# Inverse roots of a three-round attention by Newton steps on VectorE, with TensorE's fillers and the keys' statistics placed elsewhere

## What is computed

```python
def _ln(x, w, eps=1e-05):
    m = jnp.mean(x, axis=-1, keepdims=True)
    v = jnp.var(x, axis=-1, keepdims=True)
    return (x - m) * jax.lax.rsqrt(v + eps) * w

for it in range(3):
    ql = qcur[:, :, :E] @ Wlq.T + blq
    kl = kcur[:, :, :E] @ Wlk.T + blk
    vl = vcur[:, :, :E] @ Wlv.T + blv
    qs = _ln(ql, lnc_w) * tscale
    ks_ = _ln(kl, lnd_w)
    logits = jnp.einsum('bhqd,bhkd->bhqk', qs, ks_) * sm_scale
    ai = jnp.einsum('bhqk,bhkd->bhqd', jax.nn.softmax(logits, axis=-1), vl)
    iter_out = jnp.zeros_like(qcur).at[:, :, :E].set(ai)     # only the first E = 16 positions
    diff = jnp.mean(jnp.abs(iter_out - prev))
    attn_out = jnp.where(done, attn_out, iter_out)
    done = done | (diff < thr + fac * diff) & (it > 0)
    prev, qcur, kcur, vcur = iter_out, qcur + iter_out, kl, vl
```

## Time and profile before

| | us |
|---|---|
| median of 3 runs (2586.53 to 2589.68) | 2589.26 |
| profiled execution, its own time | 2587.26 |
| its span, first to last instruction | 2585.5 |
| TensorE busy (share of the span) | 2471.9 (96%) |
| VectorE | 2179.0 (84%) |
| ScalarE | 1852.1 (72%) |
| GpSimd | 1123.0 (43%) |
| opening stage, its last VectorE instruction to end | 151.4 |
| the next stage's first instructions | 151.65 |

### The profile page before, as it was taken

One profiled execution on the slowest core, in us unless ns is written; L12 is line 12 of the kernel. 1 busy time (PEld: TensorE's weight loads), 2 busy tenths in 40 slices (PEclk: granted clock), 3 DMA queues, 4 the chain that ended last, 5 costly groups with the idle time before them and its releaser, 6 DMA issues.

```text
span 2585.5 us, 56476 instructions
## 1 busy us (share of the span) xinstructions
PE 2471.9 (96%) x21670; PEld 1412.7 (55%) x21670; DVE 2179.0 (84%) x3022; ACT 1852.1 (72%) x3375; POOL 1123.0 (43%) x1436
## 2 busy tenths in 40 slices
PE   6769989999999689999999999999999999999998
PEld 4559988999999433444444434444444344444443
DVE  3458878888888789999999999998999999989992
ACT  2248768888887358777777787777777877777776
POOL 3335545555555215344344353443443534434434
PEclk9889999999999779999999999999999999999999
DMA  2015565555554677858777778597777786877762
GB/s 77 1 37 165 177 168 177 176 179 176 177 174 157 169 118 142 158 101 165 144 118 148 122 146 160 100 166 142 120 148 115 151 162 99 162 146 121 148 90 67
DMA packets 355167, 353.46 MB, mean 137 GB/s; under 512 B 112024, under 2 KB 280366, under 8 KB 354496
## 3 DMA queue, kind: packets, MB, share of 16 engines
q1 hardware_dynamic: 345794, 346.33, 61.8%
q10 hardware_dynamic: 9104, 3.51, 0.8%
HBM read 228.62 MB, written 120.06 MB: 135 GB/s over the span
## 4 chain that ended last, share of the span: by engine, by line
PE 63%; DVE 2%; ACT 1%; issue 0%; POOLq 0%; POOL 0%; ACTq 0%; DVEq 0%
PE t_r L1613 24%; PE t_y L1629 22%; PE t_a L1571 13%; PE t_a L1596 4%; DVE t_mxc L1717 2%; ACT t_prob L1656 1%; PE t_a L1583 0%; DVE t_ysw L1730 0%; POOLq L1410 0%; DVE t_o L1747 0%; POOL t_yn L1815 0%; DVE t_yT L1741 0%; ACT t_yh L1681 0%; DVE t_rec L1734 0%; ACTq L1673 0%
## 5 line engine op out<-in xcount | busy, mean ns | idle before, releaser
L1656 ACT ACTIVATE t_prob<-t_r 128x512 f32<-128x512 f32 (+1 forms) x2432 | 1217.9, 579 | 359.7 <-PE t_r L1613 342.7
L1717 DVE TENSOR_REDUCE t_mxc<-t_a 128x2 f32<-128x1024 f32 (+3 forms) x1216 | 1348.6, 1154 | 92.3 <-PE t_a L1571 92.2
L1613 PE MATMUL t_r<-t_q,t_k 109*128 109x128 bf16 (+4 forms) x4608 | 699.2, 277 | 2.5 <-ACT t_prob L1656 0.6
L1629 PE MATMUL t_y<-t_prob,t_v 128*32 128x512 f32 (+3 forms) x6144 | 628.1, 496 | 0.0
L1613 PEld LDWEIGHTS t_r<-t_q,t_k 102*128 102x128 bf16 (+1 forms) x4608 | 315.3, 98 | 440.7 <-ACT t_prob L1656 278.8
L1571 PE MATMUL t_a<-t_km,t_qm 63*128 63x128 bf16 (+4 forms) x4608 | 410.7, 279 | 28.6 <-DVE t_mxc L1717 19.6
L1794 POOL TENSOR_SCALAR_AFFINE_SELECT t_prob<-t_prob 128x512 f32<-128x512 f32 x512 | 316.6, 634 | 243.9 <-ACT t_prob L1656 235.2
L1571 PEld LDWEIGHTS t_a<-t_km,t_qm 51*128 51x128 bf16 (+1 forms) x4608 | 154.6, 95 | 302.2 <-DVE t_mxc L1717 189.2
L1815 POOL TENSOR_TENSOR t_yn<-t_ysw,t_rec 128x256 f32<-128x256 f32 x128 | 79.4, 620 | 531.3 <-DVE t_rec L1734 531.3
L1629 PEld LDWEIGHTS t_y<-t_prob,t_v 128*32 128x32 f32 x6144 | 134.5, 108 | 183.7 <-issue 114.9
L1168 POOL TENSOR_TENSOR j_part<-p_rest,j_part 128x1024 bf16<-128x1024 f32 x64 | 138.1, 2158 | 143.4 <-ACT j_part L985 143.4
(11 more groups left out here) (203 smaller groups left out, 3626.0 us busy)
## 6 DMA issues: line engine op xcount, KB each, us to landing
t_q<-scr_q SPq DMA_DIRECT2D x384, 128.0 KB
t_k<-scr_k SPq DMA_DIRECT2D x384, 128.0 KB
scr_q<-j_part SPq DMA_DIRECT2D x96, 256.0 KB, 3.4
scr_k<-j_part SPq DMA_DIRECT2D x96, 256.0 KB, 2.6
t_qm<-scr_q SPq DMA_DIRECT2D x384, 64.0 KB
t_km<-scr_k SPq DMA_DIRECT2D x384, 64.0 KB
scr_v<-j_v SPq DMA_DIRECT2D x32, 544.0 KB, 5.0
t_v<-scr_v SPq DMA_DIRECT2D x64, 272.0 KB
```

The lines of the kernel that those rows point to most:

```text
L1613: mm = pe.matmul(ring[n % RING_BANKS][:, s * w + lo:s * w + hi], k_op[z][0:deep, h0 + s, j * P:(j + 1) * P], q_op[z][0:deep, h0 + s, q0 + ...
L1629: mm = pe.matmul(ybank[32 * h:32 * h + 32, q0 - 512 * c:q0 - 512 * c + w], v[t % BUFS][:, j, h * VW:h * VW + 32], prob[:, (NQ * t + r) % S ...
L1656: nc.scalar.activation(prob[:, q % SLOTS, h0:h0 + m, 0:w], ring[n % RING_BANKS][:, 0:m * w].rearrange("p (h n) -> p h n", h=m), ACT.Exp).t ...
L1717: V.tensor_reduce(out, data, AX.X, ALU.max, negate=True).then_inc(s_au, 1)
```

## The change

The inverse roots of the start's keys and of the queries in all rounds leave GpSimd. `root(n, it)` on VectorE computes them from the bits: the float's bits, read as an integer, times -0.5 plus 1597463007 is the first guess y; three Newton steps y = y (1.5 - 0.5 v y y) follow, each of three instructions. Every instruction waits for the one before (`link` puts a semaphore between two of VectorE). GpSimd keeps only the roots of the keys of rounds 1 and 2. Besides, the order changes:

- TensorE: three fillers instead of six ahead of the start's keys' deviation; in a round, three fillers between the queries' variance and deviation instead of six; the keys' mean behind that deviation, four fillers behind it instead of five; the keys' variance behind the first turning back, eleven fillers behind it; the keys' deviation behind the second turning back.
- ScalarE: the keys' square behind its half of the first spread.
- VectorE: the queries' root, widening, normalisation and half of the spread come directly behind `eps`; the keys' centring and the remainders of the weights behind them; the keys' `eps` and the values' transpose behind the softmax's subtraction; the keys' widening behind the second spread; the keys' normalisation behind the addition to the queries.

```diff
@@ GpSimd
-            power(1, 0)
-            for it in range(ROUNDS):
-                power(0, it)
-                if it + 1 < ROUNDS:
-                    power(1, it + 1)
+            for it in range(1, ROUNDS):
+                power(1, it)
@@ TensorE
             variance(1, 0)
-            fill(6)
+            fill(3)
             deviation(1, 0)
...
                 variance(0, it)
+                fill(3)
+                deviation(0, it)
+                pe.wait_ge(s_nrm[1], it + 1)
                 if more:
-                    pe.wait_ge(s_nrm[1], it + 1)
                     mean(1, it + 1)
-                    variance(1, it + 1)
-                fill(6)
-                deviation(0, it)
-                fill(5)
-                pe.wait_ge(s_nrm[1], it + 1)
+                fill(4)
                 for half in range(2):
                     pe.wait_ge(s_qbd[half], it + 1)
...
                 turn_back(2 * it + 1).then_inc(s_sc_pe, 1)
-                fill(3)
+                if more:
+                    variance(1, it + 1)
+                fill(11)
+                for half in range(2):
+                    pe.wait_ge(s_pbd[half], it + 1)
+
+                products(vt[:, it % 2, :], pbd).then_inc(s_raw_pe, 1)
+                turn_back(2 * it + 2).then_inc(s_pv_pe, 1)
                 if more:
                     deviation(1, it + 1)
-                fill(8)
-                for half in range(2):
-                    pe.wait_ge(s_pbd[half], it + 1)
-
-                products(vt[:, it % 2, :], pbd).then_inc(s_raw_pe, 1)
-                turn_back(2 * it + 2).then_inc(s_pv_pe, 1)
                 fill(3)
@@ ScalarE
                     latent(2, it + 1)
-                    square(1, it + 1)
...
                 spread(qbd, qn, s_qbd[1])
+                if more:
+                    square(1, it + 1)
                 copy_raw(2 * it + 1)
@@ VectorE
+            def root(n, it):
+
+                y, half, var = rstd[n][:, :, :], newton[:, :, :], ve[n][:, :, :]
+                dve.wait_ge(s_ve[n], it + 1)
+                if it > 0:
+                    dve.wait_ge(s_wide[n], it)
+                link(V.tensor_scalar(y.bitcast(INT32), var.bitcast(INT32), -0.5, ROOT_GUESS, ALU.mult, ALU.add))
+                for step in range(3):
+                    link(V.tensor_tensor(half, y, y, ALU.mult))
+                    link(V.scalar_tensor_tensor(half, half, -0.5, var, ALU.mult, ALU.mult))
+                    i = V.scalar_tensor_tensor(y, half, 1.5, y, ALU.add, ALU.mult)
+                    if step < 2:
+                        link(i)
+                i.then_inc(s_rstd[n], 1)
...
             eps(1, 0)
+            root(1, 0)
             swap_v(0)
...
                 eps(0, it)
+                root(0, it)
+                widen(0, it)
+                norm(0, it)
+                dve.wait_ge(s_nrm[0], it + 1)
+                if it > 0:
+                    dve.wait_ge(s_sc_pe, it)
+                spread(qbd, qn, s_qbd[0])
                 if more:
                     centre(1, it + 1)
-                    eps(1, it + 1)
...
-                widen(0, it)
-                norm(0, it)
-                dve.wait_ge(s_nrm[0], it + 1)
-                if it > 0:
-                    dve.wait_ge(s_sc_pe, it)
-                spread(qbd, qn, s_qbd[0])
-                if more:
-                    swap_v(it + 1)
                 copy_raw(2 * it + 1)
...
                 if more:
-                    widen(1, it + 1)
+                    eps(1, it + 1)
+                    swap_v(it + 1)
                 dve.wait_ge(s_exp, it + 1)
...
                 spread(pbd, pt, s_pbd[0])
                 if more:
-                    norm(1, it + 1)
+                    widen(1, it + 1)
                 copy_raw(2 * it + 2)
...
                     V.tensor_tensor(cur[0][:, :], cur[0][:, :], ai[it][:, :], ALU.add).then_inc(s_cur[0], 1)
+                    norm(1, it + 1)
                 if it == 1:
```

More of the change, by code:

```diff
@@ L47 @@
 EPS = 1e-5
+INT32 = mybir.dt.int32
+ROOT_GUESS = 1597463007.0
 BIG = -1e30
@@ L190, in prepare @@
         neghalf = sb("p_neghalf", [P, W // P, HPC])
+        newton = sb("p_newton", [P, W // P, HPC])
         hmask = sb("p_hmask", [P, HPC])
@@ L473, in _ @@
                 turn_back(2 * it + 1).then_inc(s_sc_pe, 1)
-                fill(3)
                 if more:
-                    deviation(1, it + 1)
-                fill(8)
+                    variance(1, it + 1)
+                fill(11)
                 for half in range(2):
@@ L482, in _ @@
                 turn_back(2 * it + 2).then_inc(s_pv_pe, 1)
+                if more:
+                    deviation(1, it + 1)
                 fill(3)
```

## The result

The changed kernel takes 2570.18 us (median of 4 executions, 2567.98 to 2571.68) against 2588.01 of the kernel before beside it: a ratio of 0.9925, with a 95% interval of 0.9914 to 0.9937 (the two medians alone give 0.9931). The profiled execution took 2567.98, with a span of 2566.3.

What follows compares the result with a forecast made beforehand. The prediction took the opening stage's latency, a ring of dependent steps with the inverse root as widest link, as the bound. Savings 16.4 less 1.1 for moves and 4.5 for clock gave 10.8: 2587.3 - 10.8 + 0.9 = 2577.4 us, range 2571.5 to 2585.5.

Steps and rivals of the forecast that it cites:

- Direction and place: Opening stage, ending at 151.6 us: whatever it gains moves all that follows forward one for one; stage end expected at 140.8.
- The root: Four inverse roots on VectorE: ten dependent instructions at 0.235, 2.35 us each, bounds 2.0 to 2.95; integer reading taken as free.
- The 1.3 us: Rounds 0 and 1: part of each 4.5 us saving, from cutting the fillers ahead of the transposes from six to three.
- Start: Start's keys, root to TensorE: TensorE starts at 37.4 instead of 39.84, 2.4 us saved before any clock cost.
- Rounds 0 and 1: Queries' variance to normalisation in each of these rounds: 3.8 instead of 8.3 us, 4.5 saved in each.
- Sum less moves: Opening stage: root savings of 16.4 us less 1.1 for moved instructions, 15.3 left with the clock as it was.
- Round 2: Variance to normalisation 4.2 instead of 8.6 us, then 0.65 more ahead of the products: 5.0 saved.
- The clock: TensorE half-clock drops in the opening stage: 2.4 us at the start, 0.9 each in rounds 0 and 1, 0.3 in round 2.
- The low end: Fastest time of the range, 2571.5 us: the full 15.3 saved, 1.4 more from four roots at 2.0, and 0.9 added.
- Base: Whole kernel: profiled 2587.3 us as starting time, plus 0.9 because the mean of four runs lies that much above it.
- The exclusion of GpSimd's pow and VectorE: Softmax rival: VectorE's multiplication waits for the keys' pow, costing 3.9 us in each of two rounds; 2585.2 us, chance 0.04.
- Fillers as the bound: Opening-stage rival: fillers at half clock hold TensorE, some 14 us in a round; 2600 us with two rounds, chance 0.05.

Runs made afterwards that it cites:

- the second execution: The changed kernel run again with nothing edited, for another profiled execution: median 2570.26 us, 19.4 us saved against the kernel before.
- 3.63 or 4.85 of idle time: Changed kernel with six Newton steps instead of three (3.63): 2583.21 us; changed kernel with all roots on GpSimd's pow again (4.85): 2589.73 us.
- the wait filled to 1.04: Changed kernel with six Newton steps instead of three and nine fillers instead of three in the queries' wait: 2582.83 us.
- Roots alone: Kernel before with only the four roots moved to VectorE, its order and fillers kept: 2590.06 us, ratio interval 0.9992 to 1.0010.
- the order alone: Changed kernel with all six roots on GpSimd's pow again, the new order kept: 2589.73 us, ratio interval 0.9989 to 1.0007.

## Why the prediction was right or wrong

- **Direction and place: right.** The stage's end sets the time, what follows is unchanged (2433.75), and most of the gain lies between the variance and what waits for the root: 2.79, 4.63, 4.61 and 4.47 of the 19.1 us.
- **The root: right.** 2.25 us in ten instructions for 2.35. Nothing extra for integers. The 1.3 us that the forecast booked to the fewer fillers in rounds 0 and 1 belong to the clock as much: with six fillers and full clock these rounds lost nothing.
- **Start: 4.35 where 2.4 was summed.** From the variance's read to the transposes 2.79 were gained. The other 1.56 lie ahead of the root: 1.13 in what precedes the variance, where the 24 projection matmuls took 6.11 us in place of 7.14 in the same code, and 0.43 in variance matmuls at full clock. No edit touches what ran there, and the second execution of the same kernel had its variance's read at 33.36, not 32.06: it scatters, and the sum had no term for it.
- **Rounds 0 and 1: 4.74 and 4.16.** Sum less moves was 4.25 and 3.65 before the clock. Variance to normalisation gave 4.63 for 4.5, normalisation to products 0.14 in round 0, and the softmax lost nothing for 0.15. The 0.7 of round 1 was lost as said: the keys' normalisation stands at 94.48, ahead of the difference.
- **Round 2: 5.85 for 5.0.** 0.72 for 0.65 behind the normalisation, 4.47 for 4.4 ahead of it; the rest is 0.26 in products that run at full clock (2.01 us; 2.27 before) and 0.39 from projection to variance.
- **The clock: the step that failed.** The term of 4.5 us, taken between 0 and 8, was the larger part of the miss of 7.2. The 0.9 charged to each of rounds 0 and 1 cost nothing: in all seven traces with the new order, the fillers and a root of two or three steps no drop began in these rounds. For the start the term was right in one execution (2.3 for 2.4) and nothing in the other. For round 2 it had the wrong sign: 0.3 was charged, and the half-clock time fell from 17.1 to 10.2 us, in the second execution to 6.8. Without the charge on rounds 0 and 1 the forecast is 2575.6; with none at all, 2572.9.
- **What took the time below the range.** The low end had no clock cost in it already, and shorter roots than were measured (2.0 for 2.25). The stage gained 19.1 in the profiled execution where the sum had 15.3 before the clock; of the 3.8 more, 1.56 lie ahead of the start's root, 0.39 behind it, 1.0 in rounds 0 and 1 and 0.85 in round 2. The bound of zero for the clock was no bound: with less half-clock time than before it gave back 0.43 in the start's variance matmuls and 0.26 in the products of round 2.
- **Why there was no drop in rounds 0 and 1: open in part.** With 3.63 or 4.85 of idle time the drop was there, and with the wait filled to 1.04 it was gone. But the kernel before dropped in round 0, from 49.6 on, with no wait longer than 1.44 us. Its timeline and a stretch:

```profile
48.22 1.06 PE L384 MATMUL p_b<-p_avgh,p_sq 128*128 128x8 f32 x8 [1.44 <-ACT p_sq L515]
```

```profile
50.00:53.00 3.00, 3.00 (x8) 2.37 (x7) 2.18 (x4) 0.00 (x0) 3.00 (x2) 0.50 0.00 0
```

From the projections' end to the fillers (44.12 to 49.14) TensorE idled 2.1 us there; from the projections' end to the transposes (39.77 to 44.47) it idles 2.3 now. So shorter waits don't explain the full clock. What left this stretch is the keys' mean and a second set of eight tiny variance matmuls; that these count towards a drop is the forecast's own reading, and no run tested it.
- **Base.** 0.9 was added to the profiled time for the median. Over 21 executions in another measurement the median of the kernel before was 2589.7, 2.4 above its profiled execution. So the saving was set against too fast a kernel. That hid part of the miss: beside those 21 executions the change's median is 19.4 lower, 8.6 more than the 10.8 forecast.
- **Rivals.** The exclusion of GpSimd's pow and VectorE fell: the softmax's multiplication ran at 55.72 in its usual 0.69 us inside the pow from 54.09 to 59.52. Fillers as the bound did not occur in the change, but the experiments show what it looks like (114.00 and 120.50 in round 2). The raw copies started 2.01 us after their products, as before, and so were not late.
- **Not foreseen: the parts don't add.** Roots alone save -0.4, the order alone 0.0, both 19.4. The prediction priced roots and order as separate terms, and by its terms each would have saved some us alone. The short root needs VectorE and TensorE cleared in front of it. The new order with the long wait has the drops of rounds 0 and 1 again (from 52.4 and from 86.5), and with the short one it hasn't.

Open: whether the eight tiny variance matmuls count as idle time for the clock. No run moved only the keys' statistics out of the kernel before, or left only them in the new order.

## What to carry to other kernels

In a chain of small steps, count how long TensorE idles in each wait, and which tiny matmuls stand beside it (whether these count is open here). If that changes, the clock behind it may change too, and a forecast should let this term go both ways. Set fillers again after each such change: they must fill the wait at full clock and still end before their consumer at half clock. And when an edit has two parts, measure each alone before pricing them by a sum.

## What was not expected of the hardware

TensorE's speed and the granted clock disagree early in the span. In 19 to 24 us both kernels' records show full clock, and both are busy throughout, yet with different numbers of the same matmuls. Before, and then after:

```profile
19.00:24.00 5.00, 5.00 (x16) 4.15 (x17) 0.67 (x4) 2.21 (x4) 1.83 (x5) 1.00 0.83 258
```

```profile
19.00:24.00 5.00, 5.00 (x21) 4.31 (x22) 1.40 (x7) 2.10 (x4) 1.83 (x5) 1.00 0.87 249
```

So the clock of a stretch ahead of its first recorded change should be taken from the duration of matmuls, not from the row. Besides, the keys' widening of round 1 took 1.27 us at 88.88 beside GpSimd's memsets and 0.43 elsewhere, as a widening did before, while two-input VectorE instructions beside a pow ran at their usual speed.
